# Row sums of causal attention added up over key tiles on GpSimd before one product with ones, and two kept quarters of transposed probabilities in place of three

## The chip, the cores and the metric

The kernel runs on one core of a Trainium2 chip. The time is the device time of one execution in microseconds; the median of several executions counts. TensorE is PE here (its weight loads are PEld), VectorE is DVE, ScalarE is ACT, GpSimd is POOL and SyncE is SP.

## What is computed

Four layers are applied one after the other to x, of shape (4, 256, 32, 32) in float32, that is four images of 1024 tokens with 256 channels: L0, attention with short queries and keys; L1, group norm and full attention; L2, causal attention with eight heads of 32 channels that share one key and one value head, followed by a feed-forward part with layer norms; L3, group norm and full attention again. The change lies in L2 (and, for one buffer, in the full attention of L0, L1 and L3):

```python
sim = jnp.einsum('bhid,bjd->bhij', q, k)
sim = jnp.where(causal, neg, sim)
attn = jax.nn.softmax(sim, axis=-1)
out = jnp.einsum('bhij,bjd->bhid', attn, v)
```

So each query of each head needs the sum over the keys of exp(sim - max) times v, divided by the sum over the keys of exp(sim - max).

## The kernel before

Two chains of work are woven together on every engine. The full chain ("F" or a digit in the ORDER strings) does the attention of L0, L1 and L3 for the four images, twelve layer passes in the order of `FULL`. The causal chain ("C" or a letter a to h) does L2. For each engine ORDER is a string that says, event by event, which chain gives the next piece; the strings are the output of a planner and are written out by hand in the source. For PE a digit or letter also says at which of the eight PSUM banks (`ring`) the piece opens, so a string fixes both the order on the engine and the banks.

**The causal part of an image** has eight blocks k (`BLOCKS`): four quarters qi of 256 queries by two groups hg of four heads. Block k takes 2 (qi + 1) key tiles jt of 128 keys: 2, 4, 6 or 8 for the four quarters, 40 in an image and 160 in all. One key tile is one step:
- PE writes the scores of four heads (`causal_exponents`, L1009), 128 keys on the partitions by 4 times n queries. n is 256, and 128 for the last tile of a block, whose first half of queries lies before the keys.
- ACT takes the exponent into one of three buffers, `cprobs[:, step % 3]` (L1234), 4 x 256 elements on each partition.
- For the last two tiles of a block (the diagonal) POOL sets what lies above the diagonal to zero with an affine select (L707) and raises `diag_masked`.
- PE (`causal_values`, L1028) runs eight products from the same probabilities: for each of four heads one with the values `v2` as weights, which gives the numerators in columns 0 to 255 of the block's bank, and one with `ones` as weights, which gives the denominators, repeated over the 32 channels, in columns 256 to 511. Each head uses 32 columns of the array, and the four of a kind run side by side. Each appears in the trace as two instructions, so a step has 8 with `v` and 8 with `ones`. They come two steps (LAG) after the scores.

After a block's last step ACT copies denominators and numerators out of PSUM (L1242 `sums`, L1243 `nums`) and frees the bank; DVE (`normalise`) inverts the 256 denominators on every partition in two pieces (L1618, 128 x 128 each), multiplies (L1623), and splits the result in a high and a low part (L1624, L1625) for the output product.

POOL has besides the masks only powers of -0.5: eight for the group norms (L686) and 56 for the layer norms (`root`, L694, for which DVE waits at L1511 and L1514). It takes them in the order of the causal list.

**The full part**: for each tile of 128 queries PE makes scores (L728, L759), DVE reduces them to a row maximum (L1307, L1310, L1311), ACT takes the exponent and its row sum (L1085), DVE scales by the inverse (L1317, L1318), PE transposes (L772), ACT copies the transposed probabilities to `probsT` (L1093), and for each quarter of queries PE multiplies by the values (`full_values`, L781). `probsT` holds three quarters; quarter qi goes to place qi % 3. On PE the products of quarter qi stand before the first transposes of quarter qi + 2.

Of the kernel before, what the change touches and what calls it, by code (L numbers as in the profile page):

```python
# [41 lines left out]
        "FF4F6F012F4FFF5ac4F60F456Fca142Ff067FFF1F03efhb4F0d67bFFecaFegca4F623aa7aegc7aeFcFFfCag12adeCgcbC0FbdfFdChFf"  # L42
        "dfCbadhghfC0bdCfbceCfbdhfa2efCCaCgCFea520ecCFeccCegcgheccC0F4gcaCgC20ecCage2aCF6ea7aecfaCfc2F705bFbCCcCaChC7"
        "d20fCFbCfhFdbCFfC2aFe614F063FFF1eCFdCaC065CC1che0FFFCfba6Ff3F21a6F5edbFFaegdF1Caef1F35Fa723Faf72afda5F723Fea"
        "FfahFeace0F62eCfdhfdCaghC3F572aFadFaChdaFdCfha3F01fgchC34f7aCFdFfagFCd5a7fc7FdaFFgfCCd7CaCbf3F05a3FfC0FdffC0"
        "ceg2ef0g2aFgC406deFbC04d1CFgd0C67baFdbCFdaFfe2afFaC750cgF523ghCCFaFCfFC2h0CFd2567aC5cFCgaFbF3FfCgC123fgFb5CF"
        "gCFbCFC6Cb5ah5F1Cad515hF041Fd075Fedeb073FFaefhF1CaefF703Ff120dfbhFdFfF1hdfdaF7fdf65d3eCbg0bcdCfhbCFFgceFbCg3"
        "e3beC3FgaFbFefghCacCehahCceagce0F2heFC0Cc4F0CF2hCe0F572F4a50Fc7eC23aFeFaCeFgac4F6d70F2e67FaeCFcgFaC4F7g2C60e"
        "7bFCeFgaFeC26ae2gdaFegCFaeFhgCCa2CeChCa1F46eC0F6eCFac4gdCaC64d0gF345F730F453FFF6F014F301FFF06eCaCdCF543CC0gc"
        "b2CaedFFhF0Fc345habF7FadbeFCadF1d0c0F25aegc2ae2F67aeacgeah2eF70bCef2FbheCageC754FhcaFcCfFacaCg4Fc3a60hcheCFf"  # L50
        "cCegcgCec7cg45acFFheCCaFChC72hFe701eeC70ceFeCFgFbdfbgceC2F60hefC2aFCe0gCFegFeFgCeage0fafC05acF0hcCCfC0cC5hC0"
        "cFf7C35FaCch04bd1CfFCa340bCFfCFbCCFCg3hF025CbF347FFF5Fa1723e5FFghF06C0FFF71F350F2F4602F456F012F456FFF0F723F5"
        "67FFF0F23456FFF707FFF"),
    "ACT": (
        "FFFFCFFFCFFCCFFFCCFFFCCFFFFFFCFFFFFFFFFFFFFFFFFFFFFFFFFFFFFFFFFFFFFFFCFFFFFFFFFCCFFFFFCCFFFFFFFFFCCFFFCCCCCF"
        "FFFFCCCCCCFFCCCCCCCCCCCCCCCCFCFCCCCFCFFCCCCCFFCFCCFFCCCCCFFFCCCFFCFCCCFFFCCCCCCCCFFFFFFCCCFFCFCCFFFFCCCFFFFC"
        "FCFCCCCFFCFCFFFCFFFCCFFCCCCCCFFCCCCFFFCFCCCCCFCFFFFCCCFCFCCCCCCFFCFFFFCFCFCFCFCFFFCCFCFFCFFFCCCCCFFFCFCFCFCC"
        "CFFFFCFFFCCCCFCCFFCCCCFCCFCFFFCCFFCFFFCFFFFFFCCCCCFCFFFFFCCCCCCFFFCCFFCCCCCCCFCFCCCCCCCCCCFFCFCFCFCFFFCFFFCF"
        "FFFFFCCCCFFFFFFCCCCFFFFFCCCFFCCCCCCCCCFFFFFCFCCCFFCCCFFCFFFFFFFFFFFFFFFCCCFCFCCFFFFFCCCFCFFCCCCFCFCFFFFCCFCC"
        "FFCFCCCFCCFFCCCCFFFCCCCCCFFCFCCCCCFFFCCCCCCFFFFFFFCCCCCFFFCCCCCCCCFCFFCFCFCCFCFCCFFFCCCCFCFFCFFFCCCCCFCFFFFF"  # L60
        "CFFFFFCFFCFFFFFFFFFFFFFFFFFFFFFFFFFFFFFFFF"),
    "DVE": (
        "CFFFFCFFFFCFFCCFFCCFFCCFCFFFFFCFFFFFFFFFFFFFFFFFFFFFFFFFFFFFFFFFFFFCCFFCFFFFFCCFFCCFFFFCCFCFFFFFCCCCFFFCCCCC"
        "FFFFCCCCCFFCCCCCCCCCCCCCCCCCFCCCCCFFCCCCCCCCCCCFCCFCCFFFCCFFCCCCCCCCCCCCCCCFCCCCFFCCFCFCCCCFCCCCCCCCFFFFCCCF"
        "CCCCCCCCCFCFCFFFFCCFCCFCCCCCFFFCCCCCCCCCFCCFCFCCCCCCCCFCFCCFFCFFFCCCFCCFFCCCCCFFFCCCCCCCCFFCCCCCCCCCFCCCCCFF"
        "FCCCCCCFCCCFCFCCCCCFFFCFCFFCFFFCFCCFCCCFFCCCCCCFFCCCCFCCFCFCFCFCFCCCCFCCCCFCCFCFFFCFFFCFFFCCCFFFCCFCCCFCCCCC"
        "CCCFFCCCCCFFFCCCCFCFCCCCFCCFCFFCCFCCCCCCFCFCCFFCFCCCCCFCCCCFCFCCCCCCCCCCCCCCCCCFCCCCCFCCCCCCCCCCCCCFFCCFFCCF"
        "FFFCFCCFFFFCCCCFCCCCCFCFFCCFFCCFCCCFCFFCFCCCFCFCCCCCCCCFFFCFFFFFFCFCCCCFCCFFCCFFCCCCFFFFFFFFFFFFFFCCFCCCCCCC"
        "FFFFFFCCCCCCCCCFCCFCCCCCCCCCCFFCCFCFFFCCCCCFFCCCCCFFCFCCCCCCCFCCCCCCCCCFCCCCCFCCCCCCCFCCFCCCCFCCFCCFFCCCFCFF"
        "CFCCFFFCCCCCCCCCCFCCFCCCCCCFCCCCCFCCCCFFFCFCFCCFCCCFCCCFCCFCCFCFCCCCFFCCCCFCCCFCFFCFCCCCFCFFFFFFFFFFFFFFFFFF"  # L70
        "FFFFFFFFFFFF"),
    "POOL": (
        "FCCCCCCCCCCCCCFCCCCCCCCCCCCCCCCCCCCCCCCCCCCCCCFCCCCCCCFCCCCCCCCCCCCCCCCCCCCCCCCCCCCCFCCCCCFCCCCCCCCCCCCCCCCC"
        "CCCFCCCCCCCCCCCCCCCF"),
    "SP": (
        "FCCCCCCCCCCCCCCCCCCCCCCCCCCCCCCCCFCCCCCFFCCCCCCCCCCCCCCCCCFCFCFFFF"),
# [196 lines left out]
def causal_units():  # L273

    out = [("prep.vo1", "dve", 2), ("prep.qk1", "dve", 1), ("prep.b2", "dve", 1), ("prep.vo3", "dve", 2),
           ("prep.qk3", "dve", 1)]
    for b, e in causal_order():
        if e[0] == "values":
            if is_final(e):
                out.append((causal_name(b, e), "act", 1))  # L280
        elif e[0] not in NO_UNIT:
            out.append((causal_name(b, e), "act" if e[0] in FILLED_BY_ACT else "dve", causal_banks(e)))
    return out


def queries(k, jt):

    return QUARTER - max(jt * P - BLOCKS[k][1] * QUARTER, 0)

# [43 lines left out]
def build(nc, t):  # L333
# [6 lines left out]
    for ch, us in units.items():  # L340
        total = {"act": 0, "dve": 0}
        for i, (name, eng, _) in enumerate(us):
            chain[name], freed_by[name], fill_no[name] = ch, eng, i + 1
        for name, eng, _ in full_units(False) if ch == "f" else us:
# [16 lines left out]
    DIAG = len(diagonal)  # L361
    last_max = {e[1]: e for e in schedule if e[0] == "max"}
# [1334 lines left out]
```

## Time and profile before

| what | value |
|---|---|
| median of 3 runs | 1383.55 us (1383.23 to 1387.08) |
| the profiled execution | 1385.56 us |
| its span, first to last instruction | 1383.8 us |
| busy, PE / DVE / ACT / POOL | 93% / 63% / 43% / 7% of the span |

A span is shorter than the execution's own time by what lies before the first and after the last instruction, 1.8 us here. Busy time is the union of an engine's instructions, so instructions that overlap count once. PE's instructions are pipelined and their ends are modelled: what a group of them costs is read better from the distance between starts than from their durations.

### The profile page before, as it was taken

The numbers are of one execution on the slowest core, as the hardware profiler recorded it, in microseconds if no ns is written. First come the engines' busy times: TensorE is split into PE (matmuls) and PEld (weight loads), VectorE is DVE, ScalarE is ACT, GpSimd is POOL, SyncE is SP. The second block draws the span as 40 slices with busy tenths as digits, with TensorE's granted clock in tenths as the row PEclk, the third lists the DMA queues.
The fourth block names the chain that finished last, engine by engine and source line by source line (L and its number), as shares of the span: only waits on it lengthen the run. The fifth ranks groups of instructions, "written<-read, shape, count | busy, mean of one in ns | idle before, by whom it ended". The sixth has DMA issues, their size and how long they took to land.

```text
span 1383.8 us, 21791 instructions
## 1 busy us (share of the span) xinstructions
PE 1292.8 (93%) x8800; PEld 1011.3 (73%) x8800; DVE 866.0 (63%) x1854; ACT 593.9 (43%) x973; POOL 93.9 (7%) x134
## 2 busy tenths in 40 slices
PE   6979999889999999999999999999999999999898
PEld 5868777666678767677788667777787767768786
DVE  3634456787557587865567586776576768555451
ACT  3423343355444544444454344455325444443331
POOL 0000000110000000100100000000001000010000
PEclk9989999999999899999999999999999999999999
DMA  5000020110002010000020111000020100000000
GB/s 189 1 0 1 0 77 1 24 24 1 2 1 46 2 24 2 24 1 1 1 46 2 40 47 24 1 1 1 1 47 1 24 17 24 16 1 16 16 1 31
DMA packets 20611, 27.04 MB, mean 20 GB/s; under 512 B 3489, under 2 KB 14241, under 8 KB 20513
## 3 DMA queue, kind: packets, MB, share of 16 engines
q1 hardware_dynamic: 20512, 25.66, 6.7%
q8 instruction: 71, 1.16, 0.4%
q14 instruction: 28, 0.22, 0.0%
HBM read 8.61 MB, written 4.19 MB: 9 GB/s over the span
## 4 chain that ended last, share of the span: by engine, by line
PE 84%; DVE 8%; ACT 5%; issue 2%; DMA 0%; SPq 0%; POOL 0%; ACTq 0%; DVEq 0%
PE ring L728 28%; PE ring L781 25%; PE ring L1028 9%; PE ring L1009 5%; PE ring L992 5%; PE ring L772 5%; DVE part_max L1597 2%; ACT cprobs L1234 1%; PE ring L809 1%; PE ring L928 1%; PE ring L961 1%; PE ring L996 1%; ACT probs L1085 1%; PE ring L759 1%; DVE neg_max L1307 1%
## 5 line engine op out<-in xcount | busy, mean ns | idle before, releaser
L781 PE MATMUL ring<-probsT,vt 128*128 128x256 f32 x1536 | 361.7, 387 | 11.7 <-ACT probsT L1093 11.7
L781 PEld LDWEIGHTS ring<-probsT,vt 128*128 128x128 f32 x1536 | 290.4, 193 | 61.9 <-ACT probsT L1093 14.6
L1234 ACT ACTIVATE cprobs<-ring 128x1024 f32<-128x1024 f32 (+1 forms) x160 | 150.6, 941 | 206.1 <-PE ring L1009 205.7
L1085 ACT ACTIVATE probs<-ring,neg_max 128x1024 f32<-128x1024 f32 x96 | 107.0, 1115 | 200.3 <-DVE neg_max L1311 107.4
L1597 DVE TENSOR_REDUCE part_max<-ring 128x2 f32<-128x1024 f32 (+2 forms) x112 | 126.4, 1142 | 38.5 <-PE ring L992 24.0
L992 PE MATMUL ring<-ks,qs 96*128 96x512 f32 (+3 forms) x384 | 110.7, 385 | 15.1 <-ACT cprobs L1234 6.0
L1093 ACT COPY probsT<-ring 128x512 f32<-128x512 f32 x192 | 102.8, 591 | 26.2 <-PE ring L772 26.2
L1009 PE MATMUL ring<-qs,ks 98*128 98x512 f32 x288 | 107.5, 445 | 5.3 <-ACT probs L1085 2.5
L728 PE MATMUL ring<-h_hi,q_hi 128*128 128x512 f32 x256 | 107.4, 419 | 5.0 <-ACT cprobs L1234 2.8
L1310 DVE TENSOR_REDUCE shift_max<-ring 128x1 f32<-128x1024 f32 x64 | 78.2, 1222 | 53.2 <-PE ring L728 46.8
L772 PE MATMUL ring<-consts,probs 128*128 128x128 f32 x768 | 106.6, 280 | 5.0 <-ACT probs L1085 1.5
L772 PEld LDWEIGHTS ring<-consts,probs 128*128 128x128 f32 x768 | 90.2, 144 | 25.1 <-issue 5.8
L728 PE MATMUL ring<-h_hi,q_lo 128*128 128x512 f32 x256 | 100.4, 392 | 0.0
L728 PE MATMUL ring<-h_lo,q_hi 128*128 128x512 f32 x256 | 100.2, 392 | 0.0
L1028 PE MATMUL ring<-cprobs,v 128*32 128x256 f32 (+1 forms) x1280 | 95.9, 372 | 0.2 <-ACT cprobs L1234 0.2
L1028 PE MATMUL ring<-cprobs,ones 128*32 128x256 f32 (+1 forms) x1280 | 91.8, 359 | 0.0
L992 PEld LDWEIGHTS ring<-ks,qs 96*128 96x128 f32 x384 | 62.4, 193 | 37.3 <-issue 10.8
L694 POOL TENSOR_TENSOR rstd<-var_eps,half_neg 128x2 f32<-128x2 f32 (+1 forms) x56 | 45.4, 810 | 601.2 <-DVE var_eps L1495 601.2
L1318 DVE TENSOR_SCALAR probs<-probs,row_inv 128x1024 f32<-128x1024 f32 x96 | 72.3, 754 | 3.4
L707 POOL TENSOR_SCALAR_AFFINE_SELECT cprobs<-cprobs 128x512 f32<-128x512 f32 x64 | 42.9, 672 | 423.5 <-ACT cprobs L1234 422.9
L1009 PEld LDWEIGHTS ring<-qs,ks 98*128 98x128 f32 x288 | 48.4, 191 | 28.0 <-issue 19.5
L728 PEld LDWEIGHTS ring<-h_hi,q_hi 128*128 128x128 f32 x256 | 48.2, 188 | 22.0 <-issue 6.6
(221 smaller groups left out, 2128.2 us busy)
## 6 DMA issues: line engine op xcount, KB each, us to landing
qs<-q_hi SPq DMA_DIRECT2D x32, 128.0 KB, 2.3
qs<-q_hi SPq DMA_DIRECT2D x64, 64.0 KB, 2.0
x<-x_dram SPq DMA_DIRECT2D x3, 1024.0 KB, 6.5
qs<-q_lo SPq DMA_DIRECT2D x16, 128.0 KB, 2.3
qs<-max_rows SPq DMA_DIRECT2D x128, 2.0 KB
qs<-q_lo SPq DMA_DIRECT2D x32, 64.0 KB, 2.0
out_dram<-z SPq DMA_DIRECT2D x4, 512.0 KB, 2.8
out_dram<-x SPq DMA_DIRECT2D x4, 512.0 KB, 2.8
```

The costliest lines, as they stand in the source:

```text
L728: ins = mm(out, w, m, start=first and n == 0, stop=last and n == len(every) - 1)
L772: last = nc.tensor.transpose(o[:, j, :], probs[:, ti % 2, (TPH * hf + j) * P:(TPH * hf + j + 1) * P], ident)
L781: last = mm(o[:, ct * QUARTER:(ct + 1) * QUARTER], vt[:, j, ct * P:(ct + 1) * P], probsT[:, qi % (NQ - 1), j, :], start=j == 0, stop=j == ...
L992: last = mm(o, stack(k, a, 3 * DH, at, at + P), ks[0:3 * DH, lo:hi], start=i % own == 0, stop=not diag and i % own == own - 1)
L1009: last = mm(heads(name)[:, a:a + own, 0:n], ks[0:3 * DH + 2, jt * P:(jt + 1) * P], stack(k, slice(a, a + own), 3 * DH + 2, QUARTER - n, QU ...
L1028: last = mm(acc[DH * a:DH * (a + 1), (half + 1) * QUARTER - n:(half + 1) * QUARTER], w, causal_probs(step, n)[:, a, :], start=jt == 0 and ...
L1085: A(probs[:, ti % 2, :], flat(full_name(l, b, ("s", ti))), ACT.Exp, bias=neg_max[:, ti:ti + 1], accum_out=row_sum[:, ti:ti + 1]).then_inc( ...
L1093: nc.scalar.copy(probsT[:, ti // 2 % (NQ - 1), js, (ti % 2) * P:(ti % 2 + 1) * P], slot(name)[:, 0, :].rearrange("p (s n) -> p s n", n=P)) ...
L1234: A(causal_probs(step, n), heads(name)[:, :, 0:n], ACT.Exp).then_inc(read_done["c", "act"], 1)
L1310: full_then(v.tensor_reduce(shift_max[:, ti:ti + 1], flat(name), AX_X, ALU.max, negate=True))
L1318: v.tensor_scalar(probs[:, ti % 2, :], probs[:, ti % 2, :], row_inv[:, ti:ti + 1], None, ALU.mult).then_inc(probs_scaled, 1)
L1597: v.tensor_reduce(cols if ti < TPH else parts[:, ch, :], src[:, :, 0:n], AX_X, ALU.max, negate=True).then_inc(read_done["c", "dve"], 1)
```

## The change

The core of it: in the six blocks of an image with qi above 0 (`has_sum`), POOL adds the probabilities of the tiles jt = 0, 1, 2, ... element by element into `block_sum` (two of them, by turns, 4 x 256 elements on each partition), and PE multiplies with ones only once, from `block_sum`, after the block's last product with the values. The two blocks of the first quarter keep a product with ones per tile. An addition of a diagonal tile waits for that tile's mask, the first of a block waits until the block two sums before has been finished on PE, and every other one waits for the addition before it. The exponent of a step now waits until POOL has added what lies in its buffer from three steps before.

```diff
+            def add(b, e):
+                _, k, jt, step = e
+                n = queries(k, jt)
+                total = block_sum[:, k % 2, :, QUARTER - n:QUARTER]
+                if e in diagonal:
+                    pool.wait_ge(diag_masked, b * DIAG + diagonal.index(e) + 1)
+                else:
+                    wait_read(pool, causal_name(b, e))
+                if jt == 1:
+                    if b or has_sum(k - 2):
+                        wait_filled(pool, f"C{b}.o{k - 2}" if has_sum(k - 2) else f"C{b - 1}.o{k + K - 4}")
+                    first = causal_probs(step - 1, n)
+                else:
+                    pool.wait_ge(summed, b * ADDED + added.index(e))
+                    first = total
+                pool.tensor_tensor(total, first, causal_probs(step, n), ALU.add).then_inc(summed, 1)
...
-                for half, w in ((0, v2[:, jt, :]), (1, ones[:, 0:DH])):
-                    for a in range(4):
-                        last = mm(acc[DH * a:DH * (a + 1), (half + 1) * QUARTER - n:(half + 1) * QUARTER], w,
-                                  causal_probs(step, n)[:, a, :], start=jt == 0 and half == 0, stop=is_final(e) and half == 1)
+                for a in range(4):
+                    mm(acc[DH * a:DH * (a + 1), QUARTER - n:QUARTER], v2[:, jt, :], causal_probs(step, n)[:, a, :],
+                       start=jt == 0, stop=False)
+                if has_sum(k):
+                    if not is_final(e):
+                        return
+                    pe.wait_ge(summed, b * ADDED + added_no(exp))
+                    tiles, n = block_sum[:, k % 2, :, :], QUARTER
+                else:
+                    tiles = causal_probs(step, n)
+                for a in range(4):
+                    last = mm(acc[DH * a:DH * (a + 1), 2 * QUARTER - n:2 * QUARTER], ones[:, 0:DH], tiles[:, a, :],
+                              start=False, stop=is_final(e))
...
+                        if step < STEPS:
+                            if b:
+                                act.wait_ge(summed, b * ADDED)
+                        elif has_sum(probabilities[step - STEPS][1]):
+                            act.wait_ge(summed, b * ADDED + added_no(probabilities[step - STEPS]))
                         A(causal_probs(step, n), heads(name)[:, :, 0:n], ACT.Exp).then_inc(read_done["c", "act"], 1)
```

The end of a block changes too. ACT no longer copies anything out; DVE reads the block's bank itself: it transposes the denominators in squares of 32 x 32, so that the 32 equal copies of a denominator lie side by side, inverts one column of each square (8 elements on a partition in place of 256), transposes back from a broadcast, and multiplies the numerators out of PSUM. The bank is free after that product:

```diff
-                        nc.scalar.copy(sums[:, k % 2, :], acc[:, QUARTER:])
-                        nc.scalar.copy(nums[:, hg, token_quarter(qi)],
-                                       acc[:, 0:QUARTER]).then_inc(read_done["c", "act"], 1)
...
-                    ins = v.reciprocal(den[:, piece * P:(piece + 1) * P], den[:, piece * P:(piece + 1) * P])
+                    causal_then(v.transpose(turned_sums[:, :, :].rearrange("p s n -> p (s n)"), acc[:, QUARTER:]))
+                    causal_then(v.reciprocal(inverse[:, :], turned_sums[:, :, 0]))
+                    causal_then(v.transpose(den[:, :, :], inverse[:, :].unsqueeze(2).broadcast_to([P, TPH * 2, DH])))
...
-                    causal_then(v.tensor_tensor(nums[:, hg, to], nums[:, hg, to], den, ALU.mult))
+                    v.tensor_tensor(nums[:, hg, to], acc[:, 0:QUARTER], den[:, :, :].rearrange("p s n -> p (s n)"),
+                                    ALU.mult).then_inc(read_done["c", "dve"], 1)
```

Room for `block_sum` (8 KB on a partition) comes from `probsT`, which keeps two quarters (`NQ - 1` becomes 2, and quarter qi goes to place qi % 2). All five ORDER strings are new: PE's differs from its 195th sign on, ACT's loses 32 pieces, POOL's has 248 in place of 128 (eight of them for the full chain, as before).

## Rows read from the trace of the kernel before

**Rows 1.** The page: span, busy shares, and the chain that ended last.

```profile
span 1383.8 us, 21791 instructions
PE 1292.8 (93%) x8800; PEld 1011.3 (73%) x8800; DVE 866.0 (63%) x1854; ACT 593.9 (43%) x973; POOL 93.9 (7%) x134
PE 84%; DVE 8%; ACT 5%; issue 2%; DMA 0%; SPq 0%; POOL 0%; ACTq 0%; DVEq 0%
```

**Rows 2.** Busy time by stretch: stretch, length, engines (count), PE clock, DMA share, GB/s.

```profile
230.00:420.00 190.00, 177.59 (x1400) 127.51 (x1399) 133.04 (x283) 85.09 (x132) 17.83 (x24) 1.00 0.04 10
...
sum 1384.00, PE 1292.78 PEld 1011.28 DVE 866.00 ACT 593.93 POOL 93.89; mean PE 129.28 PEld 101.13 DVE 86.60 ACT 59.39 POOL 9.39
```

**Rows 3.** Groups by shape, PE at L1028: count | busy us, mean ns | idle before.

```profile
L1028 PE MATMUL ring<-cprobs,ones 128*32 128x256 f32 x1024 | 78.7, 379 | 0.0
...
L1028 PE MATMUL ring<-cprobs,ones 128*32 128x128 f32 x256 | 13.1, 277 | 0.0
```

**Rows 4.** Timeline of PE: start us, us, engine, line, count; end of a block.

```profile
409.66 0.40 PE L1028 MATMUL ring<-cprobs,v 128*32 128x128 f32 x8
409.88 0.40 PE L1028 MATMUL ring<-cprobs,ones 128*32 128x128 f32 x8
410.21 0.66 PE L772 MATMUL ring<-consts,probs 128*128 128x128 f32 x4
```

**Rows 5.** Timeline of PE: a step in the middle of a block.

```profile
401.84 0.64 PE L1028 MATMUL ring<-cprobs,v 128*32 128x256 f32 x8
402.30 0.61 PE L1028 MATMUL ring<-cprobs,ones 128*32 128x256 f32 x8
402.84 0.50 PE L728 MATMUL ring<-h_hi,q_hi 128*128 128x512 f32 x1
```

**Rows 6.** Groups by shape, POOL: count | busy us, mean ns | idle before.

```profile
L707 POOL TENSOR_SCALAR_AFFINE_SELECT cprobs<-cprobs 128x512 f32<-128x512 f32 x64 | 42.9, 672 | 423.5 <-ACT cprobs L1234 422.9
L694 POOL TENSOR_TENSOR rstd<-var_eps,half_neg 128x2 f32<-128x2 f32 x48 | 36.4, 759 | 440.3 <-DVE var_eps L1495 440.3
```

**Rows 7.** Groups by shape, DVE and ACT.

```profile
L1618 DVE RECIPROCAL sums<-sums 128x128 f32<-128x128 f32 x64 | 57.9, 930 | 1.1 <-ACT nums L1243 1.0
L1623 DVE TENSOR_TENSOR nums<-nums,sums 128x256 f32<-128x256 f32 x32 | 14.7, 459 | 0.4
L1317 DVE RECIPROCAL row_inv<-row_sum 128x1 f32<-128x1 f32 x96 | 15.4, 160 | 56.1 <-ACT probs L1085 55.7
...
L1243 ACT COPY nums<-ring 128x256 f32<-128x256 f32 x32 | 12.3, 385 | 0.0
L1242 ACT COPY sums<-ring 128x256 f32<-128x256 f32 x32 | 11.9, 371 | 18.5 <-PE ring L1028 18.4
...
L1318 DVE TENSOR_SCALAR probs<-probs,row_inv 128x1024 f32<-128x1024 f32 x96 | 72.3, 754 | 3.4
```

**Rows 8.** Timeline of POOL and DVE: two stretches where both work.

```profile
251.23 1.41 POOL L707 TENSOR_SCALAR_AFFINE_SELECT cprobs<-cprobs 128x512 f32<-128x512 f32 x2 [14.11 <-ACT cprobs L1234]
...
252.06 0.85 DVE L1623 TENSOR_TENSOR nums<-nums,sums 128x256 f32<-128x256 f32 x1
...
295.96 1.22 DVE L1382 TENSOR_TENSOR h_lo<-h_full,h_hi 128x1024 fp32r<-128x1024 f32 x1
...
296.00 2.26 POOL L707 TENSOR_SCALAR_AFFINE_SELECT cprobs<-cprobs 128x512 f32<-128x512 f32 x2 [10.67 <-ACT cprobs L1234]
```

**Rows 9.** Timeline of ACT: the densest row of exponents, and an image's last one.

```profile
248.67 1.02 ACT L1234 ACTIVATE cprobs<-ring 128x1024 f32<-128x1024 f32 x1 [1.39 <-PE ring L1009]
...
250.10 1.06 ACT L1234 ACTIVATE cprobs<-ring 128x1024 f32<-128x1024 f32 x1
251.34 0.60 ACT L1234 ACTIVATE cprobs<-ring 128x512 f32<-128x512 f32 x1 [0.18 <-PE ring L1009]
257.89 1.02 ACT L1234 ACTIVATE cprobs<-ring 128x1024 f32<-128x1024 f32 x1 [5.96 <-PE ring L1009]
...
406.42 0.60 ACT L1234 ACTIVATE cprobs<-ring 128x512 f32<-128x512 f32 x1 [0.41 <-PE ring L1009]
```

More of the change, by code:

```diff
@@ L46 @@
[L46 to L50, printed above, removed]
@@ L283, in causal_units, with causal_reads, has_sum, is_added @@
     return out
+def causal_reads():
+    units = {u[0]: u for u in causal_units()}
+    ends = [name for name in units if name.startswith("prep")]
+    for b, e in causal_order():
+        if e[0] == "norm" and e[2] == NORM_PIECES - 1:
+            ends.append(f"C{b}.o{e[1]}")
+        elif e[0] not in NO_UNIT and e[0] != "values":
+            ends.append(causal_name(b, e))
+    return [units[name] for name in ends]
 def queries(k, jt):
     return QUARTER - max(jt * P - BLOCKS[k][1] * QUARTER, 0)
+def has_sum(k):
+    return BLOCKS[k][1] > 0
+def is_added(e):
+    return has_sum(e[1]) and e[2] >= 1
 def causal_openings():
@@ L361, in build @@
     DIAG = len(diagonal)
+    probabilities = [e for e in schedule if e[0] == "exp"]
+    added = [e for e in probabilities if is_added(e)]
+    ADDED = len(added)
     last_max = {e[1]: e for e in schedule if e[0] == "max"}
@@ L414, in build @@
         h_full = shared("h_full", [P, CT, N], r_h + 8 * KIB)
-        probsT = shared("probsT", [P, NQ - 1, NT, QUARTER], r_t)
+        probsT = shared("probsT", [P, 2, NT, QUARTER], r_t)
         def gn_stats(l, b):
@@ L426, in build @@
         cprobs = shared("cprobs", [P, STEPS, 4, QUARTER], r_c)
+        block_sum = shared("block_sum", [P, 2, 4, QUARTER], r_b)
         qs = shared("qs", [P, HG, 4, 2 * QUARTER], r_s, F32R)
@@ L601, in qk_product, with added_no @@
             return slot(f"prep.qk{l[1]}")[:, 0, :].rearrange("p (c o) -> p c o", o=C)
+        def added_no(e):
+            return 1 + next(i for i, f in enumerate(added) if f[1] == e[1] and f[2] >= e[2])
         def stack_done(eng, b, k):
@@ L703, in causal_chain @@
                         yield
[L704 to L709 removed]
+                    elif e[0] == "exp":
+                        if e in diagonal:
+                            wait_read(pool, causal_name(b, e))
+                            d = causal_probs(e[3], P)
+                            pool.affine_select(out=d, in_=d, pattern=[[0, 4], [1, P]], compare_op=ALU.is_ge,
+                                               fill=0.0, base=0, channel_multiplier=-1).then_inc(diag_masked, 1)
+                            yield
+                        if is_added(e):
+                            add(b, e)
+                            yield
             weave(ORDER["POOL"], full_chain(), causal_chain())
@@ L781, in full_values @@
                         last = mm(o[:, ct * QUARTER:(ct + 1) * QUARTER], vt[:, j, ct * P:(ct + 1) * P],
-                                  probsT[:, qi % (NQ - 1), j, :], start=j == 0, stop=j == NT - 1)
+                                  probsT[:, qi % 2, j, :], start=j == 0, stop=j == NT - 1)
                         if ct == CT - 1 and j == NT - 1:
```

94 lines of the change are left out of this document (45 added, 49 removed).

## The prediction, made from the rows above

> **What bounds the kernel now.** I read the page first, for which engine is full and which carries the chain that ended last. PE is busy 1292.8 us of 1383.8, and the chain runs 84% on PE, 8% on DVE and 5% on ACT [rows 1]. Then busy time by stretch, since the full chain alone and the woven stretches could differ: where the first image's causal blocks run (230 to 420 us) PE has 177.59 us of 190, DVE 133.04, ACT 85.09, POOL 17.83 [rows 2]. So in the stretches that the change touches PE sets the pace, DVE is second at 70%, and POOL is nearly empty. Time taken from PE there is worth nearly its full size, unless what replaces it makes DVE or a chain of waits the bound.
>
> **What PE loses.** In the blocks with qi above 0 an image has 2 x (4 + 6 + 8) = 36 steps, 144 in all, 24 of them (one per block) with 128 queries. Each drops its product with ones; 24 products of full width from `block_sum` come in. The price comes from distances between starts, not from busy time. In the middle of a block the eight products with `v` start at 401.84, those with ones at 402.30 and the next work at 402.84 [rows 5]: the `v` group takes 0.46 and the last group 0.54, of which 0.08 is paid by whichever group comes last. A step so falls from 1.00 to 0.54: 0.46 saved. For the narrow step the starts are 409.66, 409.88, 410.21 [rows 4]: 0.55 falls to 0.33, 0.22 saved. Sum: 120 x 0.46 + 24 x 0.22 - 24 x 0.46 = 55.2 + 5.3 - 11.0 = 49.5 us. By busy time it would be more (78.7 us for 128 wide groups is 0.61 each, 13.1 for 32 narrow ones 0.41 [rows 3]; the same sum gives 69), but there the modelled ends overlap the next group. I take 49.5 and keep 69 as the far end.
>
> **What POOL gets.** 30 additions per image, 120 in all: 96 over 1024 elements, 24 over 512. The trace has no such operation. The nearest row is the mask, one input, 672 ns for 512 elements [rows 6]. At its rate 1024 elements take 1.34 us if the second input is free, 2.69 if it costs as much as the first. Two inputs are more than one, and a part of the mask's time must be fixed: I take 2.0, and 1.0 for the narrow ones. 96 x 2.0 + 24 x 1.0 = 216 us (145 to 290 by the bounds). POOL goes from 94 to some 310 us of 1343, 23%, so it is no bound by its sum.
>
> The Trainium skill (GPSIMD Engine Reference, Performance versus the Vector engine) measures 4497 ns for an addition of 2048 float32 elements; halved, that is an estimate of 2.25 us, and the 120 additions would come to 243 us.
>
> **The waits that come with it.** (a) An exponent waits for the addition that frees its buffer, and behind it on ACT stand the full chain's exponents and copies, for which PE's transposes and products wait. The densest place is the start of quarter 1 in an image, exponents at 248.67, 250.10, 251.34 and then 257.89 [rows 9]. The addition of tiles 0 and 1 would run from 249.7 to 251.7, and the exponent at 251.34 needs the buffer of tile 0: 0.4 us late, 1.0 at most, once per image. The next needs its buffer at 257.89, when POOL has long been through (mask and addition twice, until 256.0). Elsewhere the distance is larger. (b) The block's product with ones waits for the last addition. At the image's end the last exponent ends at 407.02 [rows 9]; the diagonal tile before it leaves up to 1.7 us of POOL work, then come mask 0.65 and addition 1.0: 410.4, where ones started at 409.88 [rows 4], 0.5 us late. Most blocks end with several microseconds between. (c) A power for a layer norm (0.76 us [rows 6]) can stand behind an addition, with DVE's norm waiting; and additions stand behind powers that wait for DVE. For (a) to (c) together I put 4 us on the path, 0 to 15.
>
> **What the end of a block costs.** DVE drops two inversions of 0.93 us; the multiplication stays at 0.46 [rows 7]. In come two transposes over 256 elements and an inversion of 8. No row shows a transpose; I take 0.46, as the other pass over 256 elements [rows 7], with 0.25 and 1.2 as bounds. The inversion costs 0.16 for one element and 0.93 for 128 [rows 7], so 0.2 for eight. 2.32 becomes 1.58: 0.74 x 32 = 24 us less on DVE (37 less to 24 more by the bounds). ACT drops 11.9 + 12.3 = 24 us of copies [rows 7]. The bank is freed later, after the multiplication; it is a private bank for one block at a time and the next block's first product comes steps later, so I count nothing (if it were not covered: at most the 1.6 us of DVE work, 32 times, 51 us). The two-quarter `probsT` adds no wait: PE's own order has the products of quarter qi before the transposes of qi + 2. It costs nothing.
>
> **What speaks against it: DVE and POOL share a way into SBUF.** The trace shows it both ways. DVE's multiplication at 252.06 took 0.85 us beside a mask, 0.46 on average; it ended after the mask had (252.64) [rows 7, 8]. Two masks that began just behind a DVE operation with two SBUF inputs (295.96, 1.22 us) took 2.26 us in place of 1.34 [rows 6, 8]. DVE operations with two inputs in SBUF, and those that scale or cast from SBUF to SBUF (L1318 is the largest, 72.3 us [rows 7]), are 584 in this trace with some 260 us. That is one per 2.4 us. An addition lasts 1.8 us on average, so 1 - exp(-1.8/2.4) = 53% of the 120, some 64, have one starting inside; laid on the trace behind their exponents, 65 do and hold DVE off for 82 us together (53 and 42 us at the low price, 78 and 134 at the high one). DVE grows by 82 - 24 = 58 us. The chain has 8% of 1384 on DVE, 111 us of its 866 busy: 13% of what DVE does is on the path. 58 x 0.13 = 7.5 us. For ACT the same share (69 of 594, 12%) of 24 us gives back 3.
>
> The Trainium skill (SBUF — State Buffer, SBUF: two separate sides) has the rule behind this: the pair is an exclusive lock for the whole instruction, and the later one blocks. Its GPSIMD Engine Reference even advises VectorE for element-wise work. By that rule, the trace agrees, with the 0.85 beside 0.46.
>
> **The sum.** -49.5 + 4 + 7.5 - 3 = -41 us. The profiled execution took 1385.56, so it would take 1344.6; the median is 2.0 below it: 1342.6, say 1343.
>
> **The rivals.**
> 1. *The freed time is followed by more.* Additions cost the low price, DVE and ACT are relieved by 24 us each and the woven stretches' 12 us of PE idle shrink too: 1383.55 - 49.5 - 8 = 1326. For it: DVE's inversions are long and not split. Against: every addition reads through the shared way. Chance 0.15.
> 2. *Half is given back.* DVE becomes late in the causal stretches. There it has 133 us of 190; per image it loses 6 and gets 20 of hold-offs, 147 in a stretch of 178, 83%. At the high price it is 133 + 6 + 33 = 172 of 178, and the full chain's scale and transposes wait for it. 1356 to 1379. Chance 0.18.
> 3. *No change.* PE's freed time returns as idle, since the full chain's path from scores over maximum, exponent and scale to transposes has less to hide behind: 1383. Against: PE waits little for others now (idle just before the `ones` group is 0.0 [rows 3]). Chance 0.06.
> 4. *Slower, by the lock.* If each addition keeps a DVE operation off for its whole length, since DVE comes back with the next one at once and POOL has slipped in between, hold-offs are 290 us, 72 per image: 133 - 6 + 72 = 199 us of DVE in a stretch that had 190. 4 x 9 = 36 us more: 1420, and 1388 and above in part. It decides from some 50 us per image (200 in all) on, against 82 counted. Chance 0.11.
> 5. *It doesn't do what it says*: PE runs no fewer instructions. The loop returns before ones, so no; it has no share of its own.
>
> **How the numbers follow.** The forecast (1331 to 1356, its bounds being the 0 to 15 of waits and 42 to 134 of hold-offs) has 0.50. The range goes from rival 1 to the end of rival 2, 1325 to 1379, and leaves out rivals 3 and 4, 0.17, with a little below. Faster by over 0.3% (about what a measurement of this kernel can tell from no change) is forecast, 1 and 2: 0.83; within 0.3% 0.06; slower 0.11.
>
> **What would show it.** PE: 960 instructions fewer at L1028's line (8 x 144 less 8 x 24), and PE busy near 1292.8 - 50 or up to 69 less. POOL: 120 additions; their mean alone settles 1.34, 2.0 or 2.69. DVE: the mean of L1318's line stays at 0.75 where nothing holds it; above 0.85 the lock is costly. The inversions of 0.93 gone, transposes near 0.46. PE idle before the one product with ones, and ACT idle before exponents with the addition as releaser, show the waits (a) and (b). The prediction is wrong if PE's busy share falls below 90% while DVE's rises above 75%, or if additions last over 3 us.

## The result and the profile after

The kernel after takes 1397.99 us (median, 1395.99 to 1401.89), the kernel before beside it 1383.39: the ratio is 1.0105, 95% interval 1.0084 to 1.0126. The change makes it slower by 1%, where I had forecast 1343 with 1325 to 1379 as the range.

The page of the kernel after, its span, busy shares and the chain that ended last (L1302 is the exponent, L745 the addition, L1081 the products with `v`, L1091 those with ones):

```profile
span 1394.3 us, 20193 instructions
PE 1266.1 (91%) x7840; PEld 986.5 (71%) x7840; DVE 937.5 (67%) x1886; ACT 576.2 (41%) x909; POOL 353.9 (25%) x254
PE 73%; DVE 18%; ACT 5%; issue 3%; DMA 0%; POOL 0%; SPq 0%; ACTq 0%; DVEq 0%; POOLq 0%
```

Beside [rows 1]: PE lost 960 instructions, as it should, but only 27 us of busy time; DVE, which should have become 24 us lighter by its own work, grew from 866.0 to 937.5; and its share of the chain went from 8% to 18%. Two causal stretches by busy time (columns as in [rows 2], PE, PEld, DVE, ACT, POOL, clock, DMA):

```profile
230.00:420.00 190.00, 169.31 (x1101) 121.27 (x1092) 145.36 (x279) 76.56 (x111) 80.91 (x53) 0.95 0.04 10
...
760.00:1000.00 240.00, 217.84 (x1345) 163.12 (x1344) 167.07 (x315) 97.95 (x147) 77.05 (x50) 0.94 0.06 16
```

In the first, PE is busy 169 us where it had been 178 [rows 2], DVE 145 where it had been 133, and the granted clock is 0.95 where it had been 1.00: part of the stretch ran at 1.2 in place of 2.4 GHz. Over the whole run the mean granted clock is 0.969, before it was 0.981.

The groups of POOL (count | busy us, mean ns | idle before):

```profile
L745 POOL TENSOR_TENSOR block_sum<-block_sum,cprobs 128x1024 f32<-128x1024 f32 x72 | 172.6, 2398 | 133.1 <-ACT cprobs L1302 130.2
L745 POOL TENSOR_TENSOR block_sum<-cprobs 128x1024 f32<-128x1024 f32 x24 | 57.3, 2390 | 109.2 <-ACT cprobs L1302 109.2
...
L745 POOL TENSOR_TENSOR block_sum<-block_sum,cprobs 128x512 f32<-128x512 f32 x24 | 30.8, 1285 | 2.0
```

An addition over 1024 elements lasts 2.40 us (I had taken 2.0 within 1.34 to 2.69), all 120 together 261 us. Of the waits that the additions bring, the trace shows little: exponents wait for POOL in two places, 2.6 us together, and no product with ones sat idle for it (waiting engine, what it waits for: us in total, times, longest us):

```profile
ACT cprobs L1302 <- POOL block_sum L745: 2.6, 2, 1.3
```

And the groups of DVE that show where its time came from:

```profile
L1376 DVE TENSOR_SCALAR probs<-probs,row_inv 128x1024 f32<-128x1024 f32 x96 | 81.4, 848 | 3.4
...
L1569 DVE TENSOR_SCALAR an<-xs,ln_mv,rstd 128x256 f32<-128x256 f32 x64 | 40.1, 678 | 3.7 <-POOL rstd L727 3.6
...
L1369 DVE SCALAR_TENSOR_TENSOR neg_max<-shift_max,key_bias 128x1 f32<-128x1 f32 x64 | 26.0, 407 | 2.3
...
L1679 DVE STREAM_TRANSPOSE den<-inverse 128x256 f32<-128x256 f32 x32 | 14.2, 445 | 1.1
L1676 DVE STREAM_TRANSPOSE turned_sums<-ring 128x256 f32<-128x256 f32 x32 | 14.1, 441 | 0.9 <-PE ring L1091 0.9
...
L1678 DVE RECIPROCAL inverse<-turned_sums 128x8 f32<-128x8 f32 x32 | 6.4, 201 | 0.7
```

The new end of a block costs what I had said, 0.44 for a transpose and 0.20 for the inversion. But the scaling of the probabilities lasts 0.85 us on average in place of 0.75 [rows 7], and `neg_max`, one element per partition, 0.41 where its median is 0.22. Averages hide what happens. One place, POOL, DVE and PE in the timeline of the first image's fifth and sixth blocks (start us, us, engine, line):

```profile
289.76 4.82 POOL L745 TENSOR_TENSOR block_sum<-block_sum,cprobs 128x1024 f32<-128x1024 f32 x2
...
290.82 1.30 DVE L1659 TENSOR_TENSOR cmax<-part_max 128x4 f32<-128x4 f32 x1
292.16 0.17 DVE L1664 CAST cmax_hi<-cmax 128x8 fp32r<-128x8 f32 x1
292.37 2.25 DVE L1665 COPY max_cols<-cmax_hi 128x8 f32<-128x8 f32 x1
294.53 0.15 DVE L1666 TENSOR_TENSOR max_cols<-cmax,cmax_hi 128x8 f32<-128x8 f32 x1
...
289.20 0.70 PE L1063 MATMUL ring<-qs,ks 98*128 98x512 f32 x2
294.74 0.59 PE L1003 MATMUL ring<-consts,max_cols 128*8 128x128 f32 x2 [4.84 <-DVE max_cols L1666]
```

Two additions run from 289.76 to 294.58. An operation over four elements (L1659, it joins two sets of maxima) is held until the end of the first and ends at 292.12, a copy of eight elements is held until the end of the second, and the transpose of `max_cols`, next in PE's written-out order, comes 4.84 us after PE had finished its last work. DVE's cast at 292.16 got in between, before the second addition began:

```profile
292.25 2.34 POOL L745 TENSOR_TENSOR block_sum<-block_sum,cprobs 128x1024 f32<-128x1024 f32 x1
```

Here whoever comes first has the way. The granted clock goes to its lower level of 1.2 GHz during that idle time, at 293.8, and stays there for 6.8 us; the row of this stretch (columns as in [rows 2]):

```profile
293.80:300.60 6.80, 5.86 (x25) 5.56 (x26) 5.97 (x13) 4.14 (x7) 0.79 (x1) 0.50 0.08 20
```

### The profile page after: what moved, and what is told of

Same layout as the page of the kernel before. It is cut to its first block, busy times and chain, and to the rows that moved or that the text cites. A ratio compares the mean times of both kernels' runs of the same rounds, so it can differ in the third digit from the quotient of the medians.

```text
span 1394.3 us, 20193 instructions
## 1 busy us (share of the span) xinstructions
PE 1266.1 (91%) x7840; PEld 986.5 (71%) x7840; DVE 937.5 (67%) x1886; ACT 576.2 (41%) x909; POOL 353.9 (25%) x254
## 4 chain that ended last, share of the span: by engine, by line
PE 73%; DVE 18%; ACT 5%; issue 3%; DMA 0%; POOL 0%; SPq 0%; ACTq 0%; DVEq 0%; POOLq 0%
PE ring L782 26%; PE ring L835 23%; PE ring L1081 4%; PE ring L1063 4%; PE ring L826 4%; PE ring L1046 4%; DVE part_max L1655 3%; DVE an L1569 2%; PE ring L863 1%; DVE cmax L1659 1%; PE ring L982 1%; ACT probs L1148 1%; DVE shift_max L1368 1%; PE ring L1015 1%; DVE q_lo L1346 1%
## 5 line engine op out<-in xcount | busy, mean ns | idle before, releaser
L1302 ACT ACTIVATE cprobs<-ring 128x1024 f32<-128x1024 f32 (+1 forms) x160 | 150.2, 940 | 260.8 <-PE ring L1063 257.7
L745 POOL TENSOR_TENSOR block_sum<-block_sum,cprobs 128x1024 f32<-128x1024 f32 x96 | 203.5, 2120 | 135.1 <-ACT cprobs L1302 130.2
L1081 PE MATMUL ring<-cprobs,v 128*32 128x256 f32 (+1 forms) x1280 | 97.8, 378 | 0.0
L745 POOL TENSOR_TENSOR block_sum<-cprobs 128x1024 f32<-128x1024 f32 x24 | 57.3, 2390 | 109.2 <-ACT cprobs L1302 109.2
L1376 DVE TENSOR_SCALAR probs<-probs,row_inv 128x1024 f32<-128x1024 f32 x96 | 81.4, 848 | 3.4
```

The source lines that it names most:

```text
L745: pool.tensor_tensor(total, first, causal_probs(step, n), ALU.add).then_inc(summed, 1)
L1081: mm(acc[DH * a:DH * (a + 1), QUARTER - n:QUARTER], v2[:, jt, :], causal_probs(step, n)[:, a, :], start=jt == 0, stop=False)
L1302: A(causal_probs(step, n), heads(name)[:, :, 0:n], ACT.Exp).then_inc(read_done["c", "act"], 1)
```

## The experiments

What I had to tell apart: *L*, the length of an addition during which it keeps DVE from SBUF; *W*, the extra waits in the chain, also through POOL's longer queue; *O*, the new written-out order by itself. Ratios are to the kernel before, measured on the same chip in the same series; 1% is 13.8 us. For the held-off time I take the difference of DVE's busy time between two kernels that have the same DVE instructions. Kernels in the old order have the old end of a block, those in the new order (but for one) the new end.

**Small additions in the new order.** The row sums are left out: what is not added keeps the constant that was set at the start.

```diff
-                pool.tensor_tensor(total, first, causal_probs(step, n), ALU.add).then_inc(summed, 1)
+                pool.tensor_tensor(total[:, :, n - 1:n], first[:, :, n - 1:n], causal_probs(step, n)[:, :, n - 1:n], ALU.add).then_inc(summed, 1)
```

> The kernel after with each addition on GpSimd cut to the last query of each head (4 elements instead of 1024); all its waits, its place in the queue and both orders stay. It leaves the row sums out: the denominators are those of a constant. Theory L (the additions' length, through the way into SBUF that they share with DVE, costs the gain): the hold-offs of about 99 us on DVE go, DVE's busy time falls from 937 to about 840, and the time falls by some 50 to 1340 to 1350 us. Rival W (the extra waits in the chain, whatever their length): 1375 to 1390. Rival O (the new written-out order is worse by itself): 1380 or more, still near 1390.

Measured: 1359.31 us, ratio 0.9825 (0.9793 to 0.9856). The page's busy shares:

```profile
PE 1248.6 (92%) x7840; PEld 977.2 (72%) x7840; DVE 843.1 (62%) x1886; ACT 574.6 (42%) x909; POOL 121.2 (9%) x255
```

DVE is 94 us lighter than in the kernel after with the same instructions: that is what the additions hold it off. It costs 1.0105 - 0.9825, 2.8% or 39 us. The 39 holds POOL's own lateness too; many small additions, further down, show that it has hardly a part in it. *L* is right in kind. But 1359 is 10 us above the upper end that I had written down, so *L* isn't all.

**The sums in the old order.** The kernel before, with the additions, their waits and one product with ones per block, but the old end of a block. The diff to before is shown in excerpts. PE, ACT, DVE and SP keep the strings of before; POOL's takes the additions in; one group norm power was put two places earlier, without which the engines would wait for each other in a circle.

```diff
+                        if step < STEPS:
+                            if b:
+                                act.wait_ge(summed, b * ADDED)
+                        elif has_sum(probabilities[step - STEPS][1]):
+                            act.wait_ge(summed, b * ADDED + added_no(probabilities[step - STEPS]))
                         A(causal_probs(step, n), heads(name)[:, :, 0:n], ACT.Exp).then_inc(read_done["c", "act"], 1)
...
-                for half, w in ((0, v2[:, jt, :]), (1, ones[:, 0:DH])):
...
+                    pe.wait_ge(summed, b * ADDED + added_no(exp))
+                    tiles, n = block_sum[:, k % 2, :, :], QUARTER
```

> The kernel before with the sums on GpSimd and one product with ones per block, but with the block's end as before (ACT copies out, DVE inverts 256 denominators) and with the order of before for PE, ACT, DVE and SP; only GpSimd's string is longer. Theory L: same additions, same hold-offs of 80 to 110 us, and no relief of 24 us on DVE and ACT: 1395 to 1415 us. Rival O: without the new order the 49 us of PE come through: 1340 to 1355. An order that was not made for the additions could also be worse than the new one, over 1415; then the new order is not the cause.

Measured: 1443.18 us, ratio 1.0424 (1.0390 to 1.0459). Over the upper end. The old order and the old end of a block with additions in them are far worse than the kernel after, so the sums aren't slow because of the new order alone.

**Small additions in the old order.** The same kernel with the edit of the first experiment.

> As the run with the old order, but with each addition cut to 4 elements (the row sums are left out). Theory L: about 50 us below its neighbour with full additions, 1340 to 1350. Rival W: no more than 15 us below it. Beside the kernel with small additions in the new order it says what the order is worth when nothing is held off: equal within 5 us if rival O is wrong.

Measured: 1351.78 us, ratio 0.9765 (0.9738 to 0.9791). 6.6% or 91 us lie between whole and small additions here, on 122 us of hold-offs (DVE's busy time is 988.4 and 866.6). So the same additions cost 91 us here and 39 with the new order and the new end. It is also 7.5 us below the small additions in the new order (1359.31), where equal within 5 us was to speak against *O*: that is a first sign that the new order costs something. And beside the kernel before, PE's lighter work is worth 32 us here (1 - 0.9765).

```profile
PE 1287.5 (89%) x7840; PEld 999.7 (69%) x7840; DVE 988.4 (69%) x1854; ACT 595.7 (41%) x973; POOL 354.7 (25%) x254
```

These are the shares with whole additions. Part of the 91 is the clock: PE's busy time is 36 us more than with small additions (1251.9), for the same instructions, and the mean granted clock is 0.953 beside 0.978.

**Ones per tile in the new order.** The kernel after without additions.

```diff
-                if has_sum(k):
-                    if not is_final(e):
-                        return
-                    pe.wait_ge(summed, b * ADDED + added_no(exp))
-                    tiles, n = block_sum[:, k % 2, :, :], QUARTER
-                else:
-                    tiles = causal_probs(step, n)
+                tiles = causal_probs(step, n)
```

> The kernel after without the additions: ones are multiplied once per tile again, as before; the new order and the new end of a block (DVE transposes, no copies on ACT) stay. Theory L: PE has its 49 us again, nothing is held off, DVE has 24 us less: 1375 to 1390. Rival O: the order's loss stays and PE's 49 us come back on top, 1420 or more. Should it be below 1375, the new end is worth something by itself.

Measured: 1403.37 us, ratio 1.0133 (1.0111 to 1.0154). Neither number: too high for *L* alone, too low for *O* alone. Beside the small additions it gives PE's saving in this order, with the waits and the 28 us of small additions in it: 1.0133 - 0.9825, 3.1% or 43 us; PE's busy time is 1293.0 and 1248.6, 44 us.

**The work of before in the new order.** The kernel before with the strings of after (32 pieces put back on ACT, each as soon as it is due; POOL's without the additions).

```diff
     "SP": (
-        "FCCCCCCCCCCCCCCCCCCCCCCCCCCCCCCCCFCCCCCFFCCCCCCCCCCCCCCCCCFCFCFFFF"),
+        "FCCCCCCCCCCCCCCCCCCCCCCCCCCCCCCCCFCCCCFCFCCCCCCCCCCCCCFCCCCFCCFFFF"),
...
```

> The kernel before, with its own end of a block and its own products with ones, in the new written-out order (32 pieces put back on ACT, additions taken from GpSimd's string). Theory: the new order costs by itself some 20 us when nothing is added up (that is where the run with ones per tile in the new order went): 1400 to 1415. Rival: it was the new end of a block that cost those 20 us: 1380 to 1390.

Measured: 1408.71 us, ratio 1.0165 (1.0147 to 1.0184). As the theory had it: the new order costs 1.65%, 23 us, when the old work is done in it. The new end of a block gives back 0.3%, 4 us (1.0165 to 1.0133); the intervals overlap, so this isn't clear of noise. This string for ACT has its 32 pieces where I put them, so a little of the 23 us may be theirs.

**Many small additions.** Each whole addition becomes eleven of 4 elements (six for the narrow ones). The row sums are left out.

```diff
+                for i in range(1, 12 if n > P else 7):
+                    last = pool.tensor_tensor(total[:, :, n - i:n - i + 1], first[:, :, n - i:n - i + 1],
+                                              causal_probs(step, n)[:, :, n - i:n - i + 1], ALU.add)
+                last.then_inc(summed, 1)
```

> The kernel after with each addition of 1024 elements replaced by eleven of 4 elements in a row (six for the narrow ones): GpSimd is as long at it (0.2 us each, some 2.3 us), but never keeps the way into SBUF for longer than 0.2 us. It leaves the row sums out. Theory L (DVE is held off for the rest of a long instruction): DVE's hold-offs fall from 99 us to under 30, and the time stays close to the run with one small addition, 1355 to 1370 us. Rival W2 (what counts is that GpSimd's queue is 2.4 us later with masks, sums and powers): near the full additions, 1385 to 1400.

Measured: 1360.05 us, ratio 0.9816 (0.9801 to 0.9831), the same as with one small addition. POOL's queue is nearly as late as with whole additions (205 us of them where the whole ones have 261 and the single small ones 28):

```profile
L747 POOL TENSOR_TENSOR block_sum<-block_sum,cprobs 128x4 f32<-128x4 f32 x936 | 158.0, 216 | 146.1 <-ACT cprobs L1306 141.5
L747 POOL TENSOR_TENSOR block_sum<-cprobs 128x4 f32<-128x4 f32 x264 | 47.2, 226 | 112.5 <-ACT cprobs L1306 112.5
```

DVE is busy 845.6 us, 2.5 above the single small ones. So in the new order *W* falls: lateness of POOL by 1.5 us per addition ((205 - 28) / 120, where whole ones are 1.9 later) costs nothing that can be measured. What costs there is that one instruction keeps DVE off for long. It wasn't run in the old order.

**Additions cut into four**, one per head. Everything is computed.

```diff
-                pool.tensor_tensor(total, first, causal_probs(step, n), ALU.add).then_inc(summed, 1)
+                for i in range(0, 4, 1):
+                    last = pool.tensor_tensor(total[:, i:i + 1, :], first[:, i:i + 1, :],
+                                              causal_probs(step, n)[:, i:i + 1, :], ALU.add)
+                last.then_inc(summed, 1)
```

> The kernel after with each addition cut into four, one per head (256 elements each, same sums, same waits). GpSimd is longer at it, at an estimated 0.15 us for each cut (2.9 us in place of 2.4), but a DVE instruction that comes in between waits 0.7 us at most. Theory L: hold-offs fall from 99 us to 40 to 60, time 1370 to 1390. If cutting doesn't help, since DVE meets each piece anew, 1395 or more.

Measured: 1374.47 us, ratio 0.9911 (0.9889 to 0.9932). Faster than before and after, with all the work done. A piece lasts 0.76 us; POOL is busy 414 us, 60 more than after; DVE is at 895.9, 53 above the small additions. Though POOL's additions are longer in sum than the whole ones, the loss is 12 us beside the small ones where theirs is 39, which again speaks against *W* in this order:

```profile
PE 1259.4 (92%) x7840; PEld 983.0 (71%) x7840; DVE 895.9 (65%) x1886; ACT 575.7 (42%) x909; POOL 414.3 (30%) x614
```

**Additions cut into eight** (one head, 128 queries).

```diff
+                for i in range(4):
+                    for c in range(0, n, P):
+                        last = pool.tensor_tensor(total[:, i:i + 1, c:c + P], first[:, i:i + 1, c:c + P],
+                                                  causal_probs(step, n)[:, i:i + 1, c:c + P], ALU.add)
+                last.then_inc(summed, 1)
```

> The kernel after with each addition cut into eight (one head, 128 queries each, about 0.43 us each by the narrow quarters of the run before, 3.4 us together; the narrow ones in four). Theory L: a DVE instruction waits 0.45 us at most; hold-offs 30 to 45 us and 1365 to 1373. If GpSimd's longer total or the number of meetings sets the price, 1375 or more.

Measured: 1376.15 us, ratio 0.9930 (0.9911 to 0.9949). Hold-offs fell to 38 us (DVE 880.7) as forecast, but the time didn't follow: it is on the side of the other reading, 1375 or more because POOL's longer total sets the price. The intervals of four and eight pieces overlap, so they can't be told apart. POOL now has 385 us of additions (0.48 us each), and it stands in the chain with 4%:

```profile
PE 73%; DVE 13%; ACT 6%; POOL 4%; issue 3%; DMA 1%; SPq 0%; ACTq 0%; DVEq 0%; POOLq 0%
```

Exponents wait for POOL 10.9 us in six places here, 6.6 us in three with four pieces. So finer cuts seem to trade hold-offs for POOL's own lateness; four pieces do as well as eight.

**Additions cut into four in the old order.** The kernel with the sums in the old order, with the edit of the cut into four.

> The sums in the order of before with the old end of a block, each addition cut into four. The whole additions cost 91 us there (1443.18 beside 1351.78 with small ones). Theory L: the price goes with what DVE is held off for; in the new order cutting took 99 us of hold-offs to 57 and the price from 38 to 14. So here 1443 less 60%: 1380 to 1395. If the old order with its less idle PE profits more, under 1374, and it is the fastest that computes everything.

Measured: 1401.81 us, ratio 1.0128 (1.0078 to 1.0178). A miss on the high side; three of the four runs took 1400 to 1404 us, the fourth 1415 at a mean granted clock of 0.919. Hold-offs are as in the new order (DVE 921.5, 55 above the small ones), yet these additions cost 3.6% or 50 us beside the small additions' 0.9765, and in the new order 0.9% or 12. The waits for POOL say why hold-offs alone don't give the price. First the cut into four in the new order, then here:

```profile
ACT cprobs L1305 <- POOL block_sum L746: 6.6, 3, 2.9
...
ACT cprobs L1290 <- POOL block_sum L731: 21.0, 8, 4.5
PE ring L1069 <- POOL cprobs L746: 4.3, 2, 2.2
PE ring L1079 <- POOL block_sum L731: 4.3, 3, 1.8
```

In the old order exponents wait 21.0 us for additions, and PE 8.6 us for masks and sums, of which the new order's trace has none among PE's waits. With whole additions it is the same in kind: 12.3 us of exponents in the old order, 2.6 in the new one. So *W* is refuted in the new order and not in the old one, where POOL's lateness and the hold-offs weren't separated. What the new order does for the additions seems in part to be that POOL is in time.

**Setting constants in place of additions.** Three settings of the same elements (0.97 us each), one after the other, and one small addition. The row sums are left out.

```diff
+                for i in range(3):
+                    done = 3 * (b * ADDED + added.index(e)) + i
+                    if done:
+                        pool.wait_ge(cleared, done)
+                    pool.memset(total, 1.0).then_inc(cleared, 1)
```

> The kernel after with each addition replaced by three settings of the same 1024 elements to a constant (0.9 us each, GpSimd writes and does not read) and one addition of 4 elements; it leaves the row sums out. The Trainium skill (SBUF — State Buffer, SBUF: two separate sides) says that a DVE operation with two SBUF inputs is blocked only by a GpSimd operation that reads SBUF, and one in a 2-port mode by any. So the small two-input ones (cmax L1660, neg_max L1370) should keep 0.16 and 0.22 us in all cases, while the scaling of an and probs is held off as with whole additions, up to 0.9 us each: hold-offs 15 to 30 us, 1360 to 1372. If writes block all alike, hold-offs of 40 us and more and 1370 to 1385; if a setting blocks nothing, 1360.

Measured: 1374.42 us, ratio 0.9900 (0.9874 to 0.9927), two us over the expected span; the hold-offs are 39 us (DVE 882.2), also above it. The time lies in the range of the reading that writes block all alike (1370 to 1385) and the hold-offs just under its 40 us, so these two decide nothing; single operations do. The lines named there are L1667 and L1377 in this kernel. Their minimum, median and maximum in ns:

```profile
L1377 DVE SCALAR_TENSOR_TENSOR neg_max<-shift_max,key_bias x64: 219/220/303, 108.3 to 1349.4; 128x1 f32<-128x1 f32 x64
...
L1667 DVE TENSOR_TENSOR cmax<-part_max x48: 160/161/278, 263.6 to 1210.8; 128x2 f32<-128x2 f32 x32, 128x4 f32<-128x4 f32 x16
...
L1577 DVE TENSOR_SCALAR an<-xs,ln_mv,rstd x64: 395/412/1197, 161.8 to 1273.4; 128x256 f32<-128x256 f32 x64
```

and the first of them in the kernel after:

```profile
L1369 DVE SCALAR_TENSOR_TENSOR neg_max<-shift_max,key_bias x64: 219/220/2311, 107.2 to 1371.7; 128x1 f32<-128x1 f32 x64
```

Beside additions, `neg_max` with its two SBUF inputs takes up to 2.31 us; beside settings never more than 0.30, in the same order. Of its 64, 14 began while a setting ran, and those took 0.22 us; so did 19 of `cmax`, with 0.16 us. The 0.30 and the 0.28 were beside masks, which read. The scaling with one input, SBUF to SBUF, is held off by both (up to 1.20 us here, with settings of 0.97). One two-input row seems to speak against it, the subtraction into `max_cols`:

```profile
L1674 DVE TENSOR_TENSOR max_cols<-cmax,cmax_hi x32: 153/161/899, 208.9 to 1211.9; 128x8 f32<-128x8 f32 x32
...
291.28 1.96 POOL L751 MEMSET block_sum<- 128x1024 f32 x2
...
292.29 0.98 DVE L1673 COPY max_cols<-cmax_hi 128x8 f32<-128x8 f32 x1
292.37 0.90 DVE L1674 TENSOR_TENSOR max_cols<-cmax,cmax_hi 128x8 f32<-128x8 f32 x1
```

Each of its eight long ones begins 0.08 us behind a copy that a setting holds off, and ends with that copy: it stood behind it in DVE's queue.

**The additions with no use of them.** The kernel before with whole additions, the waits, the old order, and ones multiplied per tile.

```diff
+                if has_sum(k) and is_final(e):
+                    pe.wait_ge(summed, b * ADDED + added_no(exp))
                 tiles = causal_probs(step, n)
```

> The kernel before with the additions on GpSimd (whole ones), all their waits and the order of before, but PE multiplies with ones once per tile as before and nobody uses the sums. It shows what the additions cost when PE gives up nothing. Theory L: the same hold-offs of about 130 us; as PE is fuller here, a little less of them reaches the end: 1383 plus 70 to 100 us, 1450 to 1485. Rival: PE's work hides them, and with sums it was PE that became idle: under 1430.

Measured: 1456.33 us, ratio 1.0503 (1.0483 to 1.0524). It is inside the expected span. DVE's busy time is 979.4 us, 113 above before, and the kernel is 70 us longer although PE has all its work. The additions cost 70 us before anything is gained by them, hold-offs and waits for POOL together (exponents wait 10.0 us for it here).

**Two quarters alone.** Only the buffer's places.

```diff
-        probsT = shared("probsT", [P, NQ - 1, NT, QUARTER], r_t)
+        probsT = shared("probsT", [P, 2, NT, QUARTER], r_t)
...
-                                  probsT[:, qi % (NQ - 1), j, :], start=j == 0, stop=j == NT - 1)
+                                  probsT[:, qi % 2, j, :], start=j == 0, stop=j == NT - 1)
...
-                    nc.scalar.copy(probsT[:, ti // 2 % (NQ - 1), js, (ti % 2) * P:(ti % 2 + 1) * P],
+                    nc.scalar.copy(probsT[:, ti // 2 % 2, js, (ti % 2) * P:(ti % 2 + 1) * P],
```

> The kernel before with the one edit that transposed probabilities of two quarters are kept, not three. All theories: nothing waits for it, so no difference, ratio 0.998 to 1.002.

Measured: 1383.31 us, ratio 0.9985 (0.9975 to 0.9996), at the edge of no difference and not slower. The buffer is no part of the loss.

## Why the prediction was wrong, step by step

From before to after by steps that each have two runs, in the new order:

| step | runs | ratio | us |
|---|---|---|---|
| the new order, old work | before to before_new_order | 1.0000 to 1.0165 | +23 |
| the new end of a block | to tile_ones_new_order | 1.0133 | -4 |
| one product with ones per block, with all waits | to tiny_new_order | 0.9825 | -43 |
| POOL later by 1.5 us per addition | to many_tiny | 0.9816 | -1 |
| whole additions, which hold DVE off | to after | 1.0105 | +40 |

Each ratio has an interval of 2 to 4 us to either side, so the steps of -4 and -1 are not clear of noise. The sum had -41, measured are +15. Of the 56 us between, the hold-offs' price makes 29.5 (40 for 10.5), the order 23, PE's saving 6.5; the rest nearly cancels.

- *PE's saving.* 49.5 forecast from distances between starts, 43 measured in the new order (44 in busy time), and 32 in the old one. Right in kind and somewhat too high; the far end of 69 from summed busy times was clearly too much.
- *The waits (a) to (c).* 4 us put down; in the trace after, exponents wait 2.6 us for POOL and PE's products with ones not at all. Right within its bounds.
- *POOL's price.* 2.0 taken, 2.40 measured, inside 1.34 to 2.69. The estimate of 2.25 us from the figure of the Trainium skill (GPSIMD Engine Reference, Performance versus the Vector engine) was nearer than my middle.
- *The end of a block.* 0.74 us less on DVE per block, by means of 0.44, 0.20, 0.45 and 0.42 us it is 2.32 to 1.51, 0.81. Right. Its effect on the time, 4 us and not clear of noise, agrees with the 3 for ACT and 3 for DVE (24 x 0.13) in the sum.
- *Hold-offs.* 82 us counted with the additions at 2.0 and 134 at 2.69, 94 measured with 2.40. Right in size.
- **What they cost at the end: the step that failed.** I had multiplied by 0.13, DVE's share of the chain over its busy time, and got 10.5 us for the 82. The runs say 39 to 40 of 94 in the new order (0.4). In the old one the additions cost 91 us with hold-offs of 122, and 70 with 113 when PE keeps all its work, but there the waits for POOL are in the price too. That the average share of DVE work on the chain is 13% says at most what it is worth to make all of DVE a little slower. A hold-off is up to 2.2 us at one place. How much room a step has was not measured; I take it that 2.2 us often use it up, and then the rest is on the path: the 4.84 us at 289.90 are an example, where an operation of 0.17 us for which PE's next piece waits became one of 2.25. Behind such idle time the clock went to its lower level, which an estimate by shares doesn't see: (1 - 0.969) x 1394 = 43 us of missing clock after, 26 before. PE's busy time after is 17.5 us more than with small additions (1266.1 and 1248.6, granted clock 0.969 and 0.982) for the same instructions, so the clock can hold up to nearly half of the 40.
- **What the sum left out: the order.** I had taken the five new strings as free, only as the carrier of the change. They cost 23 us with the old work. What they seem to buy: whole additions cost 40 us in them and 91 in the old ones. That would make the 23 us the price of living with the additions, paid in another place. But the old order was only run with the old end of a block, on which DVE spends 23.5 us more (866.6 and 843.1 with small additions), so the order's part in the difference isn't shown by itself. Nor are the effects additive: with small additions the new order and the new end together lie only 7.5 us above the old ones.

My own signs of a wrong forecast didn't come: PE's busy share is 91% and not below 90%, DVE's 67% and not above 75%, an addition 2.40 us and not over 3. Signs by shares and means missed a loss that lies in single places, as the sum did.

Rival 4 had the mechanism and the sign (slower, since the lock holds DVE off) with 0.11. Its own account of how was off: it made DVE full in the causal stretches, from 199 us of work in 190, and needed hold-offs of 200 us. DVE is at 145 of 190 there; over the stretch it was late, not full. Rival 2's time, half given back, is what cutting in four gives: 1374.

Open: which property of the new order costs the 23 us. It wasn't tried in parts. And why four-piece additions with the same 55 us of hold-offs cost 12 us in one order and 50 in the other: the longer waits for POOL are seen in the trace, how much of the 38 us they, the slack and the end of a block each make isn't. Many small additions in the old order, and additions in the new order with the old end, would tell; neither was run.

## What to carry to other kernels

An engine with 7% of busy time isn't free room if its instructions keep a neighbour from memory: price a long instruction on it by what it blocks at single places, not by the neighbour's mean share of the path. Where such work must go there, cut it: four pieces of 0.76 us cost 12 us where one of 2.40 cost 39, though their sum is longer. That held where the neighbours rarely waited for the engine itself; where they did, in the old order, cutting still left 50 of 91 us. And in a kernel whose order is written out by hand or by a planner, run the old work in the new order and the new work in the old one before saying what a change is worth.

## What the runs showed of the hardware

DVE operations of 0.16 to 0.75 us lasted up to 2.9 us beside a GpSimd addition, and small ones as much as large ones. Only those with two inputs in SBUF and the copies, casts and scalings from SBUF to SBUF were affected; reductions out of PSUM (1.22 us, at most 1.23) and 32 x 32 transposes (0.44 us, at most 0.45; nine of those from SBUF began during an addition) were not. Settings of constants on GpSimd held off the second kind but not the first, except where one of the first stood directly behind one of the second. The Trainium skill (SBUF — State Buffer, SBUF: two separate sides) states just this distinction, with the lock kept for the whole instruction; the runs agree, by at most 0.30 us for `neg_max` in the run with settings and 2.31 in the one with additions. I hadn't expected that eight pieces of 0.48 us would be no better than four of 0.76, nor that a float32 transpose in squares would be as cheap from PSUM (0.441 us for 256 elements) as from SBUF with a broadcast input (0.445).
